# Weight parts of the streamed feed-forward: seven places side by side, loaded in three transfers

## The reference

```
q_emb = relu(cond @ W3 + b3)                       # a gate per batch, 512 wide
y  = relu((64 * x + x.sum(axis=1, keepdims=True)) * q_emb[:, None, :] @ W2 + b2)
w_up   = ((codes - 7.5) * scale per 64).T          # 512 x 2048, 4-bit codes
y1 = relu(y @ w_up + b_up + y @ lora_a @ lora_b)   # 2048 wide
w_down = ((codes - 7.5) * scale per 64).T          # 2048 x 512
out = x + y1 @ w_down + b_down + y1 @ lora_a2 @ lora_b2
```

## Time and profile before

| | |
|---|---|
| median of 3 runs | 750.98 us (750.44 to 751.84) |
| the profiled execution | 750.74 us |
| its span, first to last instruction | 748.8 us |
| outside the span | 1.9 us |
| PE busy | 734.6 us, 98% |
| PE's granted clock | 1.0 in all 40 slices |
| DMA, mean over the span | 227 GB/s |

### The profile page before, as it was taken

One profiled execution on the slowest core, in us unless ns is written; L12 is line 12 of the kernel. 1 busy time (PEld: TensorE's weight loads), 2 busy tenths in 40 slices (PEclk: granted clock), 3 DMA queues, 4 the chain that ended last, 5 costly groups with the idle time before them and its releaser, 6 DMA issues. The chain is left out here.

```text
span 748.8 us, 9579 instructions
## 1 busy us (share of the span) xinstructions
PE 734.6 (98%) x3248; PEld 607.3 (81%) x3248; DVE 554.4 (74%) x726; ACT 420.7 (56%) x727; POOL 78.6 (11%) x68
## 2 busy tenths in 40 slices
PE   6999999999999999999999999999999999999998
PEld 5778888888878888888888888888888888888886
DVE  5998667878958497768767787767776977757596
ACT  5954384765643475858556275666656353534540
POOL 0255433242520000000000000000000000000000
PEclk9999999999999999999999999999999999999999
DMA  9979969888455896665507897656515696666663
GB/s 273 315 259 285 348 183 288 271 261 270 147 183 186 318 356 225 229 184 185 189 9 260 278 392 227 225 197 196 183 57 189 220 377 229 191 192 192 196 197 126
DMA packets 92386, 170.19 MB, mean 227 GB/s; under 512 B 8563, under 2 KB 25203, under 8 KB 91827
## 3 DMA queue, kind: packets, MB, share of 16 engines
q1 hardware_dynamic: 91474, 168.46, 68.4%
q10 hardware_dynamic: 864, 1.13, 0.6%
HBM read 129.71 MB, written 40.89 MB: 228 GB/s over the span
## 5 line engine op out<-in xcount | busy, mean ns | idle before, releaser
L1165 PE MATMUL ps<-x_hi,ring 128*128 128x512 f32 x672 | 261.6, 389 | 0.2
L1167 PE MATMUL ps<-x_hi,ring 128*128 128x512 f32 x672 | 261.4, 389 | 0.0
L1166 PE MATMUL ps<-x_lo,ring 128*128 128x512 f32 x672 | 261.4, 389 | 0.0
L1165 PEld LDWEIGHTS ps<-x_hi,ring 128*128 128x128 f32 x672 | 126.1, 188 | 27.4 <-ACT ps L519 1.0
L1167 PEld LDWEIGHTS ps<-x_hi,ring 128*128 128x128 f32 x672 | 126.1, 188 | 26.2
L1166 PEld LDWEIGHTS ps<-x_lo,ring 128*128 128x128 f32 x672 | 126.1, 188 | 26.0
L402 ACT ACTIVATE xt<-xt,gated,gate_n 128x64 f32<-128x64 f32 x216 | 75.2, 435 | 34.9 <-DVE gated L764 34.9
L511 ACT ACTIVATE f<-ps,bias 128x512 f32<-128x512 f32 x96 | 64.9, 691 | 41.6 <-PE ps L1167 41.6
L955 DVE TENSOR_TENSOR x_lo<-x_sum,x_hi 128x512 fp32r<-128x512 f32 (+1 forms) x96 | 76.7, 819 | 4.2 <-ACT x_hi L549 3.4
L876 DVE TENSOR_TENSOR ps<-s,ps 128x512 f32<-128x512 f32 x48 | 33.3, 694 | 49.5 <-PE ps L1167 49.2
L913 DVE TENSOR_TENSOR res<-ps,res 128x512 f32<-128x512 f32 x72 | 48.3, 687 | 20.5 <-PE ps L1167 20.2
(11 more groups left out here) (86 smaller groups left out, 1013.5 us busy)
## 6 DMA issues: line engine op xcount, KB each, us to landing
ring<-made_w SPq DMA_DIRECT2D x336, 256.0 KB, 3.8
made_w<-made SPq DMA_DIRECT2D x16, 1280.0 KB, 6.0
xt<-in_x SPq DMA_DIRECT2D x32, 256.0 KB, 6.1
code<-in_codes SPq DMA_DIRECT2D x16, 512.0 KB, 8.5
scale<-made_s SPq DMA_DIRECT2D x16, 512.0 KB, 8.1
res<-in_x SPq DMA_DIRECT2D x4, 2048.0 KB, 9.7
made_w<-plain SPq DMA_DIRECT2D x64, 128.0 KB, 6.4
out<-res SPq DMA_DIRECT2D x12, 512.0 KB, 5.9
```

Source lines behind the costliest of these rows:

```text
L1165: pe.matmul(dest, w_hi, a_hi, start=start, stop=False, skip_group_check=True)
L1166: pe.matmul(dest, w_hi, a_lo, start=False, stop=False, skip_group_check=True)
L1167: return pe.matmul(dest, w_lo, a_hi, start=False, stop=stop, skip_group_check=True)
```

## The change

The weights' DRAM tensor is laid out with a unit's seven parts side by side in each partition's row, and a ring buffer's parts stand at the same places as in DRAM (`W_PLACE`: M5, M2, M1, M6, M7, M3, M4 at 0 to 6). A unit is loaded with three transfers instead of seven: places 0 and 1 (M5, M2; 512 KB), places 5 and 6 (M3, M4; 512 KB), places 2 to 4 (M1, M6, M7; 768 KB). Each waits for the last of the products that read one of its places: M2, M3 and M6. A product waits for its group's semaphore. The stores into `made_w` are the same in number; their rows in DRAM are now 14 KB apart, and the five parts of `made` are contiguous within one (10 KB).

```
+W_GROUP = [slice(0, 2), slice(5, 7), slice(2, 5)]
+GROUP_OF = {M5: 0, M2: 0, M3: 1, M4: 1, M1: 2, M6: 2, M7: 2}
+GROUP_LAST = [M2, M3, M6]
...
-        made_w = nc.dram_tensor("made_w", [UNITS, 7, P, 4 * P], F32, kind="Internal").ap()
+        made_w = nc.dram_tensor("made_w", [UNITS, P, 7, 4 * P], F32, kind="Internal").ap()
...
-        w_loaded = [[sem(f"w_loaded{v}_{o}") for o in range(7)] for v in range(2)]
+        w_loaded = [[sem(f"w_loaded{v}_{g}") for g in range(3)] for v in range(2)]
...
-        def occupant_done(eng, s, n, o):
+        def occupant_done(eng, s, n, g):
 
             if n >= 2 or s > 1:
                 before, s0 = (slots(s)[n - 2], s) if n >= 2 else (slots(s - 1)[16 + n], s - 1)
                 if before[0] != "W":
-                    eng.wait_ge(prod[o], chain_no(s0, before) + 1)
+                    eng.wait_ge(prod[GROUP_LAST[g]], chain_no(s0, before) + 1)
                 elif before[1] == 0:
-                    if o < 6:
-                        wait_step(eng, s0 + 1, KD + o // 2)
-                    else:
-                        eng.wait_ge(prod[o], chain_no(s0, slots(s0)[n - 4]) + 1)
-                elif o < 2:
+
+                    wait_step(eng, s0 + 1, KD + (0, 2, 2)[g])
+                elif g == 0:
                     wait_step(eng, s0 + 1, 2 * KD - 1)
                 else:
-                    eng.wait_ge(prod[o], chain_no(s0, slots(s0)[n - 4]) + 1)
-            elif n == 0 and o < 6:
-                wait_step(eng, 1, KD + o // 2)
-            elif n == 1 and o < 2:
+                    eng.wait_ge(prod[GROUP_LAST[g]], chain_no(s0, slots(s0)[n - 4]) + 1)
+            elif n == 0:
+                wait_step(eng, 1, KD + (0, 2, 2)[g])
+            elif g == 0:
                 wait_step(eng, 1, 2 * KD - 1)
-            elif n == 1 and o < 6:
+            else:
                 eng.wait_ge(tile_done, 4 * UNITS)
...
-                        dest = made_w[uid(FIRST[u]), 5 + a, :, 2 * P * h:2 * P * h + 2 * P].rearrange("p (q c) -> p q c", q=2)
+                        dest = made_w[uid(FIRST[u]), :, 5 + a, 2 * P * h:2 * P * h + 2 * P].rearrange("p (q c) -> p q c", q=2)
...
-                sp.dma_start(made_w[uid(FIRST[u]), 0:5].rearrange("c p v -> p c v"),
+                sp.dma_start(made_w[uid(FIRST[u]), :, 0:5],
...
-                for o in range(7):
-                    occupant_done(sp, s, n, o)
-                    sp.dma_start(ring[n % 2][:, o].rearrange("p h v -> p (h v)").bitcast(F32),
-                                 made_w[uid(unit), W_PLACE[o]]).then_inc(w_loaded[n % 2][o], 16)
+                for g, places in enumerate(W_GROUP):
+                    occupant_done(sp, s, n, g)
+                    sp.dma_start(ring[n % 2][:, places].rearrange("p o h v -> p o (h v)").bitcast(F32),
+                                 made_w[uid(unit), :, places]).then_inc(w_loaded[n % 2][g], 16)
...
-                for k, (n, o) in enumerate(((12, M5), (12, M3), (12, M7), (13, M5))):
+                for k, (n, o) in enumerate(((12, M2), (12, M6), (12, M7), (13, M2))):
...
-                pe.wait_ge(w_loaded[v][o], 16 * ring_round(s, n))
+                pe.wait_ge(w_loaded[v][GROUP_OF[o]], 16 * ring_round(s, n))
...
-                    w = ring[v][:, o, :, q * P:(q + 1) * P]
+                    w = ring[v][:, W_PLACE[o], :, q * P:(q + 1) * P]
```

## The result

The changed kernel takes 763.21 us (median of 5 runs, 760.39 to 764.07) against 751.06 us before on the same chip: a ratio of 1.0152, 95% interval 1.0136 to 1.0168. It is slower, as forecast, but by 12 us instead of 3.3.

What follows compares the result with a forecast made beforehand. PE, busy 98% of the span, was taken to bound the kernel, with no load late. Slot 16's 2.1 us plus the block starts' 1.2 made 3.3 on 750.74: 754.0 us, range 752.2 to 756.6.

Steps and rivals of the forecast that it cites:

- What bounds the kernel: PE is busy 98% of the span, no weight load is late, so fewer transfers have nothing to win.
- Part 1: Issue instructions on SP: 336 issues become 144, costed at nothing since SP waits between them anyway.
- Part 2: Stores in block 0: longer contiguous rows, taken as nothing; bounds 3.8 us less and 0.5 us later.
- the sign that I had set: Opening: same within 0.5 us; the first block shifting by over 1 us would prove the stores' estimate wrong.
- rival 2: Block 0: stores end earlier, PE's four waits fall; not slower, 749.0 at best, 750.5 for half; chance 0.08.
- Part 3: Ordinary slots: loads wait for later products but stay covered, M4's by some 5 us; no late load.
- Part 4: Slot 16, after the W slots, blocks 1 and 2: M4's load late, +2.1 us, 1.5 to 3.5.
- Part 5: Start of blocks 1 to 3: M4's part lands later in a full queue, +1.2 us, bounds 0 and 3.6.
- the lead: Blocks 2 and 3: slot 1's M1, M7, M6 all go at M6's time, 1.0 us net, bounds 0.6 and 1.3.
- The size of pieces: Block starts: larger rows land sooner, giving back 0.6 us in each of three blocks.
- Rival 1: W-slot transitions are late but block starts are not; 752.8 us (752.2 to 753.5); chance 0.25.
- Rival 3: Block starts worse than costed: slots 2 and 3 wait in all three blocks, upper bounds, 756.8 us; chance 0.07.

Runs made afterwards that it cites:

- e5_four: The changed kernel with four transfers: M4 alone and first with its own wait, M5 and M2, M3 alone, M1 with M6 and M7; 753.71 us, ratio 1.0029.
- e1_layout: The kernel before with only the DRAM layout changed, still seven transfers with their old waits; 754.42 us, ratio 1.0033.
- e2_old_layout: The changed kernel with the old DRAM layout and old stores, so the grouping alone; 764.05 us, ratio 1.0161.

## Why the prediction was wrong in size

- **What bounds the kernel** held: fewer issues won nothing. SP stands waiting for products 409.8 us instead of 317.
- **Part 1** held. With M4 on time, 192 transfers (e5_four) and 336 (e1_layout) give the same blocks, 501.1 and 501.0 us.
- **Part 2, the stores, 0 us with bounds of 3.8 less and 0.5 more, failed.** It cost 4.0 us in the profiled execution (3.8 in e1_layout, 2.1 in e5_four, without the slow clock). I reasoned that PE's waits there were ended by engines, not by transfers. That was true and no protection, since the engines' own order against each other hangs on when a store lands. The faster store made it slower. By the sign that I had set, a shift of over 1 us, part 2 is wrong. It is also what became of rival 2: its condition came (the stores land in 5.8 us instead of 6.0), and the time went the other way.
- **Part 3** held: no late load in ordinary slots.
- **Part 4, slot 16, +2.1 us**, measured 2.8. The place and the mechanism were right. The load landed in 3.8 and 3.7 us instead of 3.4. Some 0.2 us of that go with the 768 KB that follow 0.4 us behind it; I had looked only at what stands ahead. An estimate by the fit of the Trainium skill ("DMA: Bandwidth & Descriptors", Anatomy of one DMA), 3.2 us, is further off.
- **Part 5, block starts, +1.2 us, is the step that failed most**: 5.2 measured, beyond my bound of 3.6. Two faults. I worked out slot 3 and gave slot 2 no working of its own, only a share of the 0.8 in block 3. Slot 3 had the smaller slack before (0.9, 2.5 and 2.2 us against 1.6, 3.5 and 3.4). But 4.2 of the 4.8 us of waits are at slot 2 (once slot 2 has waited, slot 3 has its slack shifted along). And the lead, M6's transfer, was mis-sized: from 3.2 and 2.9 us to 5.0 and 5.3, so 1.8 and 2.4 instead of 1.0. The 768 KB take 4.4 by themselves, the stores behind them give the rest. Slot 2 of block 3 shows both. Before, M4's part was issued 3.6 us behind M6's, at 599.7, and landed 6.4 us later, at 606.1, 3.4 us ahead of PE. In the changed kernel its group was issued 4.7 us behind the 768 KB, at 611.9, and took 10.9: 5.6 us more in all, and 2.2 too late. The lines of before:

```profile
L313 SPq DMA_DIRECT2D ring<-made_w x1: 1186/1186/1186, 599.7 to 599.7; - x1
...
DMA to landing us min/median/max: 6.4/6.4/6.4
...
609.52 0.39 PE L1165 MATMUL ps<-x_hi,ring 128*128 128x512 f32 x1
```

- **The size of pieces** was worth 3.0 us over the blocks (e2_old_layout against the changed kernel), where I had 1.8.
- **Sum**: 8.0 in the blocks, 4.0 in the opening and 1.2 by chance make 13.2, against 3.3. Rival 1 is out, since the block starts are late. Rival 3 had both slots waiting in all three blocks; that is nearly what came (slot 3 of block 3 was on time), and it had 0.07. Its price was too low as well: 6.1 us for both places, where 8.0 came, and nothing for the opening. It is also not the sum of the upper bounds that it claims to be: part 4's is 3.5, not 2.5, which gives 757.8. Rival 2's 750.5 for half the gain should be 750.9. Neither slip changes the answer.

## What to carry to other kernels

When transfers are grouped, each consumer inherits the last wait and the last byte of its group. Work out the slack of the first consumer at every irregular place, and of each slot behind a backlog, not only of the one with the least slack before. Take the part that is needed first out of the group, with its own wait and ahead of the others: one more transfer for each unit bought back 8 us. And a stage whose engines are interleaved by chance can lose to a faster transfer; a wait that fixes the order of two engines on a shared port makes it independent of that. Look first at which of the two another engine waits for.

## What was not expected of the hardware

- A DVE product of 8 columns took 1.15 us instead of 0.17 when it started 0.16 us after a POOL sum of 1.3 us. A store's landing 0.2 us sooner was enough to bring it about, and with three such products some 2.1 us of the run's time followed.
- PE's granted clock fell to 0.5 for some 3 us after three waits of together 1.9 us within 3 us of time, in some runs and not in others of the same kernel. In e5_four, with three waits no shorter (0.94, 0.15 and 0.85 us), it did not fall in the profiled execution:

```profile
160.00:164.00 4.00, 3.10 (x13) 1.00 1.01 328
164.00:168.00 4.00, 4.00 (x19) 1.00 0.96 281
```

- A 768 KB load followed in the queue by stores to DRAM landed in 5.0 and 5.3 us, without them in 4.4. Why block 1's queue delay differs from run to run stays open.
